# Row gathers of an edge stage released by another table, in a ring of 49 slots instead of 40

## The chip, the core and the metric

One core of a Trainium2 chip runs the kernel. The metric is the time of one execution on the device in microseconds (us). Engines are named as in the profile: PE is the matrix engine (TensorE), PEld its weight loads, DVE is VectorE, ACT is ScalarE, POOL is GpSimd, SP is SyncE, which here only issues transfers (DMAs).

## The reference

A graph layer on 3125 nodes of 256 features with 50000 edges sorted by destination, then a mixer and a layer of 16 experts. What matters here is the graph part, cut to it:

```python
xn = layernorm(x)
h   = einsum('nf,hfd->hnd', xn, W)                      # 8 heads
e   = leaky_relu(a_s[:, src] + a_d[:, dst], 0.2)         # a score for each edge and head
# for each head h_h, e_h with its gate g_h:
m   = segment_max(e_h, dst)
ex  = exp(e_h - m[dst])
den = segment_sum(ex, dst)
out = segment_sum(h_h[src] * (ex / den[dst])[:, None], dst)
acc = acc + g_h * out
# + bias, residual, layernorm, Wo; + linear attention on xn; then top-2 of 16 experts, layernorm
```

The destinations are drawn as 3125 times a squared uniform number, so that small node numbers have many edges and large ones few: windows of 16 nodes at the high end hold a little over 100 edges each, the lowest one over 3000.

## The kernel before

**Stages.** (1) The node stage normalises x, computes projections and scores of the nodes, and writes for each node a row of 272 numbers to DRAM (`node_rows`: the features, a one, the source scores of 8 heads). Ahead of it DVE works out, from the ends of the edge chunks, the tables that the edge stage goes by. (2) The edge stage sums over the edges. (3) A third stage reads the sums back and applies W, the layernorm and the expert choice. (4) The experts, and (5) an end.

**The edge stage, about 155 to 861 us.** The 50000 edges, from the highest destination down, are cut into 391 chunks of 128. A window is 16 nodes. A step is one chunk against one window: 586 steps, in 37 groups of 16 (592). Where nodes have few edges a chunk crosses into the next window often (some 1.8 steps for each chunk at the start), where they have many it rarely does (about 1.0 at the end). So a group uses 8 to 9 new chunks at the start and 14 to 15 at the end.

- POOL gathers the rows of each chunk's 128 source nodes by an indirect DMA (L735, 391 of them) into a slot of the ring `rows`, chunk number modulo `RING` = 40. `FLY` = 4 are in flight; before gather k POOL waits until gather k-4 has landed and counts it in `fetched` (L726), and then until the semaphore `prod`, which counts finished products, has reached `free_at[k]` (L732 to L734).
- ACT's `copy_as` (L907 to L914) waits on `fetched` for the last chunk of a group and copies the 16 scores' columns out of `rows` (`asb`). It runs two groups ahead of the products.
- ACT, DVE and PE turn these into exponentials by a chain of small steps, one group ahead. DVE's `spread` (L816, two per group) multiplies them out into the weights `pw`.
- PE's `product` (L1045, a step in two passes) multiplies `pw` with the chunk's rows into one of four PSUM banks `pO`; DVE's `accumulate` (L832, one per step, 592) adds it to the step before and keeps it in `acc`. PE needs the bank that DVE frees. SP stores `acc` to DRAM (L1131), 8 steps at a time in 4 parts, out of three buffers.

On each engine the order of the work is written out by hand: `groups([...])` lists stages with their lag in groups, and each engine runs through its list. There is no scheduler.

**When a gather is released.** `ends[:, 1, j]` is the number of the last step that uses chunk j, `ends[:, 2, j]` is j. PE adds 2 groups (32) to `prod` before its first product, and 1 at the start. The table is made at L491 to L493 of the node stage by DVE, on one partition: gather k may go when the product of step (last step of chunk k-4) - 48 is done (`LEAD` = 48), and not before the last product that uses chunk k-40, whose slot it takes. Some gathers at the start need no product at all.

**The read-back of maxima.** At the end of the edge stage SP loads the maxima of all steps into `ml` (L1146), and DVE makes `has` and `mm_` of them (L859, L860), which PE turns (L1093) and DVE scans. `ml`, `has` and `mm_` are buffers of their own for the whole edge stage, 5.8 KB in each partition. `gad`, of the same shape as `mm_`, is only used at the stage's start, and `picks`, of 900 numbers, only from stage 3 on.

## Time and profile before

| | us |
|---|---|
| median of three runs | 1581.97 |
| the three runs | 1574.44, 1581.97, 1582.84 |
| the profiled execution, its time | 1577.83 |
| its span in the trace | 1575.5 |
| node stage, to the first gather | 0 to 155.5 |
| edge stage, first product to last | 191 to 852 |
| third stage | about 865 to 1236 |
| experts, and the end | about 1236 to 1575 |

The stages follow each other; a stage cannot start before the data of the one before it is in DRAM. So the length of the edge stage goes into the total as it is. The profile cuts time into windows and tells for each engine the busy time and the number of instructions; in the edge stage POOL's count is the number of gathers, since it does nothing else there.

### The profile page before, as it was taken

Reading aid. Unit: us, or ns where it says so; the run is one execution under the profiler, and the core shown is the slowest. Engines: PE = TensorE matmul, PEld = TensorE weight load, DVE = VectorE, ACT = ScalarE, POOL = GpSimd, SP = SyncE. Lnnn points to the kernel's source line nnn. Section 1 sums busy time; section 2 is a strip of 40 time slices with the busy share of each in tenths; the row PEclk is TensorE's granted clock in tenths of the full one; section 3 lists DMA queues with packets and bytes.
Section 4 is the critical chain, followed back from the end, with each engine's and each line's share of the span. In section 5 each row is a group of like instructions: output and inputs, shape, how many; then the busy total and the mean of one; then the engine's idle time right before and its main releaser. Section 6 shows DMA issues by size and latency. Waiting matters only on the chain. (4 is left out here: it accounts for less than half of the span.)

```text
span 1575.5 us, 31018 instructions
## 1 busy us (share of the span) xinstructions
PE 1209.0 (77%) x6344; PEld 975.2 (62%) x6345; DVE 1004.9 (64%) x2859; ACT 504.2 (32%) x1977; POOL 690.7 (44%) x784
## 2 busy tenths in 40 slices
PE   4996689898888777677666299999991699999700
PEld 4774466666665555554444298888871689999600
DVE  6555378887777656666567468989975234444367
ACT  3452233332332222221121446555531123232200
POOL 1001655555556556556640246767663011111264
PEclk9998599999999888777888599999995799999955
DMA  5142677777777667666656833334323972222155
GB/s 184 46 88 79 131 214 231 223 234 220 218 230 224 195 189 216 193 203 191 175 178 165 262 117 134 134 133 141 133 72 118 325 252 70 70 70 70 61 163 153
DMA packets 219593, 256.19 MB, mean 163 GB/s; under 512 B 57269, under 2 KB 193336, under 8 KB 216024
## 3 DMA queue, kind: packets, MB, share of 16 engines
q1 hardware_dynamic: 177464, 140.79, 28.4%
q0 software_dynamic: 31088, 104.05, 23.0%
q10 hardware_dynamic: 10928, 10.12, 2.1%
q8 instruction: 37, 0.61, 0.2%
q14 instruction: 76, 0.62, 0.1%
HBM read 139.95 MB, written 114.93 MB: 162 GB/s over the span
## 5 line engine op out<-in xcount | busy, mean ns | idle before, releaser
L735 POOL DMA_INDIRECT rows<-node_rows,srcT x391 | 389.0, 995 | 272.4 <-PE pO L1045 132.6
L1045 PE MATMUL pO<-rows,pw 128*128 x1184 | 352.7, 428 | 67.5 <-issue 31.1
L832 DVE SCALAR_TENSOR_TENSOR acc<-acc,rsc,pO 128x257 f32<-128x257 f32 x592 | 281.7, 476 | 140.4 <-PE pO L1045 51.4
L1045 PEld LDWEIGHTS pO<-rows,pw 128*128 128x128 f32 x1184 | 223.1, 209 | 120.6 <-issue 93.1
L1377 PE MATMUL pW_<-W_again,aT 128*128 128x256 f32 x800 | 181.5, 380 | 0.4 <-DVE res L1444 0.4
L1377 PEld LDWEIGHTS pW_<-W_again,aT 128*128 128x128 f32 x800 | 148.7, 191 | 18.8 <-DVE res L1444 0.5
L1865 POOL DMA_DIRECT2D ys_rows<-ye x66 | 35.8, 542 | 235.5 <-DVE ye L1816 235.5
L1755 ACT ACTIVATE hT<-pHe,b 128x128 f32<-128x128 f32 x264 | 75.5, 368 | 188.3 <-PE pHe L1781 172.0
L1781 PEld LDWEIGHTS pHe<-xeT,w1e 128*128 128x128 f32 x1056 | 131.0, 196 | 7.1 <-DVE w1e L1806 2.8
L1781 PE MATMUL pHe<-xeT,w1e 128*128 128x128 f32 x1056 | 131.7, 279 | 3.2 <-DVE xeT L1799 3.2
L1790 PE MATMUL pYe<-w,hT 128*128 x528 | 125.4, 380 | 2.1 <-issue 1.3
L1428 DVE SCALAR_TENSOR_TENSOR own<-AG,al,own 128x256 f32<-128x256 f32 x200 | 111.1, 570 | 7.6 <-ACT own L1314 3.6
L1790 PEld LDWEIGHTS pYe<-w,hT 128*128 128x128 f32 x528 | 95.3, 191 | 13.4 <-issue 3.1
L914 ACT ACTIVATE asb<-rows 128x8 f32 x592 | 75.7, 209 | 75.9 <-issue 37.8
L816 DVE TENSOR_TENSOR pw<-pexp,eq 128x1024 f32<-128x1024 f32 x74 | 87.1, 1219 | 0.0
L1314 ACT ACTIVATE own<-xna,al 128x256 f32 (+1 forms) x200 | 82.2, 500 | 3.6 <-DVEq L1553 3.6
L1366 PE MATMUL pa<-cst,own 128*128 128x128 f32 x400 | 53.7, 292 | 36.7 <-DVE own L1428 36.7
L1799 DVE COPY xeT<-pXe 128x256 f32<-128x256 f32 x66 | 28.1, 425 | 84.3 <-PE pXe L1771 84.3
L1806 DVE COPY w1e<-w 128x1024 f32 x66 | 45.8, 694 | 51.8 <-issue 42.0
L1366 PEld LDWEIGHTS pa<-cst,own 128*128 128x128 f32 x400 | 49.2, 154 | 38.3 <-issue 33.9
L1288 POOL DMA_INDIRECT xs_rows<-ysc,slot_x x50 | 50.2, 1003 | 23.7 <-issue 11.3
L1874 POOL DMA_INDIRECT w1e<-ys_rows,slot x50 | 48.4, 968 | 25.4 <-issue 15.6
(332 smaller groups left out, 1968.3 us busy)
## 6 DMA issues: line engine op xcount, KB each, us to landing
agg_rows<-acc SPq DMA_DIRECT2D x296, 256.0 KB
w<-in_ffn_w SPq DMA_DIRECT2D x32, 512.0 KB, 5.6
xe<-xs_rows ACTq DMA_DIRECT2D x66, 128.0 KB, 2.1
ys_rows<-ye POOLq DMA_DIRECT2D x66, 128.0 KB, 2.0
rows<-node_rows,srcT POOLq DMA_INDIRECT x391
node_rows<-xna SPq DMA_DIRECT2D x25, 136.0 KB
xna<-in_x SPq DMA_DIRECT2D x5, 640.0 KB, 11.7
mix_rows<-hx SPq DMA_DIRECT2D x25, 128.0 KB
```

The source lines that it names most:

```text
L735: pool.indirect_dma_start(rows[:, k % RING, :], None, node_rows[:, :], at_row(srcT[:, k:k + 1])).then_inc(s_rows[k % len(s_rows)], 16)
L816: dve.tensor_tensor(pw[:, i, :, :].rearrange("p s (d h) -> p s d h", h=H), pexp[:, g % V2, s, :].unsqueeze(2).to_broadcast([P, HG, DW, H]) ...
L832: dve.scalar_tensor_tensor(out=acc[:, k % V3, s % HG, 0:D + 1], in0=before, scalar=rsc[:, g % V2, s:s + 1], in1=pO[n % PB][:, 0:D + 1], op ...
L914: ins = act.activation(asb[:, g % V2, s, :], rows[:, ds(at[s], 1), AS:AS + H].rearrange("p c h -> p (c h)"), ACT.Copy)
L1045: pe.matmul(pO[n % PB][:, 0:D + 1], pw[:, s // HG, s % HG, :], rows[:, ds(at[s % 4], 1), 0:D + 1].rearrange("p c f -> p (c f)"), start=Tru ...
L1314: ins = act.activation(own[:, c, h, :], tile(xna, t, 0, D), ACT.Copy, scale=al[:, 1, t, h:h + 1] if isinstance(t, int) else al[:, 1, ds(t, ...
L1366: mm = pe.transpose(pA[i][:, k * P:(k + 1) * P], own[:, c, n // KD, (n % KD) * P:(n % KD + 1) * P], ident)
L1377: mm = pe.matmul(pW[:, 0:D], aT[:, c, n, :], W[:, n % KD, n // KD, :], start=(n == 0), stop=(n == H * KD - 1))
L1428: ins = dve.scalar_tensor_tensor(out=own[:, c, h, :], in0=AG[:, c, h, :], scalar=al[:, 0, t, h:h + 1] if isinstance(t, int) else al[:, 0, ...
L1755: ins = act.activation(hT[:, c % 2, f, :], pH[c % 2][:, f * P:(f + 1) * P], ACT.Relu, bias=b1[:, ds(e, 1), f:f + 1].rearrange("p e f -> p ...
L1781: mm = pe.matmul(pH[c % 2][:, f * P:(f + 1) * P], w1e[:, c % S3, k, f * P:(f + 1) * P], xeT[:, c % 2, k, :], start=(k == 0), stop=(k == KD ...
L1790: mm = pe.matmul(pY[c % 2][:, 0:D], hT[:, c % 2, f, :], of_expert(w2, e, f), start=(f == 0), stop=(f == FK - 1))
```

## The change

The ring gets 49 slots. The table is made by three operations where there was one: each chunk takes a quarter of a step off the release, so that gather k may go when the product of step (last step of chunk k-4) - 48 - (k-4)/4 is done. The rule on the slot stays, now with chunk k-49. To make room `ml` and `has` stand in `picks` and `mm_` stands in `gad`. The slot numbers come from the same table made on the host, modulo 49.

```diff
-RING, FLY, LEAD, AHEAD = 40, 4, 48, 2
+RING, FLY, LEAD, AHEAD = 49, 4, 48, 2
+EARLIER = 0.25
...
-                    line.do(dve.tensor_scalar(may_go[:, FLY:CHUNKS], ends[:, 1, 0:CHUNKS - FLY], float(2 + AHEAD * G - LEAD), 1.0, ALU.add, ALU.max))
+                    line.do(dve.tensor_scalar(may_go[:, FLY:CHUNKS], ends[:, 2, 0:CHUNKS - FLY], -EARLIER, float(2 + AHEAD * G - LEAD), ALU.mult, ALU.add))
+                    line.do(dve.scalar_tensor_tensor(out=may_go[:, FLY:CHUNKS], in0=may_go[:, FLY:CHUNKS], scalar=0.0, in1=ends[:, 1, 0:CHUNKS - FLY], op0=ALU.add, op1=ALU.add))
+                    line.do(dve.tensor_scalar(may_go[:, FLY:CHUNKS], may_go[:, FLY:CHUNKS], 1.0, None, ALU.max))
                     line.do(dve.scalar_tensor_tensor(out=may_go[:, RING:CHUNKS], in0=ends[:, 1, 0:CHUNKS - RING], scalar=2.0 + AHEAD * G, in1=may_go[:, RING:CHUNKS], op0=ALU.add, op1=ALU.max))
                     line.do(dve.tensor_copy(free_at[:, FLY:CHUNKS], may_go[:, FLY:CHUNKS]))
...
-            ml = sb("ml", [P, SJ, DW, H + 1], ctx=ctx)
-            has = sb("has", [P, SJ, DW], ctx=ctx)
-            mm_ = sb("mm", [P, SJ, P], ctx=ctx)
+            spare = picks[:, :, :].rearrange("p t r -> p (t r)")
+            ml = spare[:, 0:SJ * DW * (H + 1)].rearrange("p (j d c) -> p j d c", d=DW, c=H + 1)
+            has = spare[:, SJ * DW * (H + 1):SJ * DW * (H + 2)].rearrange("p (j d) -> p j d", d=DW)
+            mm_ = gad
```

No engine's order changes; what changes in it stands on DVE, early in the node stage, ahead of `steps_in`, for which PE waits. `may_go` is the table before it is rounded into `free_at`. Before:

```order
L488 TENSOR_SCALAR rowc<-cs 128x5
L491 TENSOR_SCALAR may_go<-ends 1x387
L492 SCALAR_TENSOR_TENSOR may_go<-ends,may_go 1x351
L493 CAST free_at<-may_go 1x387
L495 TENSOR_TENSOR cs<-cs 128x5
```

and now:

```order
L489 TENSOR_SCALAR rowc<-cs 128x5
L492 TENSOR_SCALAR may_go<-ends 1x387
L493 SCALAR_TENSOR_TENSOR may_go<-may_go,ends 1x387
L494 TENSOR_SCALAR may_go<-may_go 1x387
L495 SCALAR_TENSOR_TENSOR may_go<-ends,may_go 1x342
L496 CAST free_at<-may_go 1x387
L498 TENSOR_TENSOR cs<-cs 128x5
```

Two operations on one partition have come in between; all else on every engine stands in the same row. How many gathers are released while a group's products run, worked out from the two tables and the drawn destinations:

| products of groups | 0-3 | 4-7 | 8-11 | 12-15 | 16-19 | 20-23 | 24-27 | 28-31 | 32-33 | 34-36 |
|---|---|---|---|---|---|---|---|---|---|---|
| before (28 need no product) | 34 | 35 | 37 | 40 | 42 | 46 | 48 | 52 | 28 | 1 |
| now (32 need no product) | 39 | 41 | 39 | 38 | 40 | 43 | 47 | 52 | 20 | 0 |

## Rows read from the trace of the kernel before

**Rows 1.** The page: busy time of each engine, and the chain that ended last.

```profile
PE 1209.0 (77%) x6344; PEld 975.2 (62%) x6345; DVE 1004.9 (64%) x2859; ACT 504.2 (32%) x1977; POOL 690.7 (44%) x784
...
PE 16%; issue 2%; DVE 2%; DMA 1%; DVEq 1%; POOL 1%; ACTq 0%; ACT 0%; SPq 0%; POOLq 0%
```

**Rows 2.** Windows of four groups each (the last two: two and three), busy us.

```profile
core 0: us, PE busy (x) PEld busy (x) DVE busy (x) ACT busy (x) POOL busy (x), PEclk, DMA share, GB/s
191.00:258.70 67.70, 59.20 (x280) 42.53 (x279) 51.35 (x140) 21.00 (x118) 39.05 (x39) 0.96 0.73 212
258.70:322.10 63.40, 57.47 (x277) 41.56 (x277) 51.65 (x140) 21.30 (x123) 35.21 (x35) 0.97 0.77 228
322.10:387.50 65.40, 57.80 (x278) 41.54 (x277) 51.52 (x141) 21.14 (x119) 37.87 (x37) 0.97 0.76 222
387.50:454.60 67.10, 58.19 (x277) 41.11 (x276) 51.41 (x140) 21.40 (x122) 38.92 (x40) 0.97 0.76 225
454.60:529.10 74.50, 59.47 (x278) 42.72 (x277) 51.56 (x141) 22.43 (x126) 42.85 (x43) 0.92 0.73 220
529.10:606.80 77.70, 63.80 (x264) 45.33 (x263) 51.25 (x136) 20.47 (x115) 46.19 (x46) 0.85 0.67 196
606.80:684.60 77.80, 55.08 (x221) 40.35 (x221) 49.44 (x124) 18.16 (x105) 47.72 (x49) 0.81 0.70 206
684.60:769.40 84.80, 57.63 (x221) 41.15 (x221) 50.04 (x124) 17.48 (x103) 49.67 (x52) 0.76 0.64 189
769.40:814.80 45.40, 27.78 (x112) 20.32 (x111) 24.75 (x62) 9.28 (x55) 27.02 (x28) 0.80 0.68 200
814.80:852.30 37.50, 30.88 (x138) 21.86 (x137) 30.37 (x73) 6.86 (x38) 0.95 (x1) 0.96 0.53 131
```

**Rows 3.** Waits of DVE in the second window: total, times, longest, us.

```profile
DVE acc L832 <- PE pO L1045: 3.5, 5, 2.0
```

**Rows 4.** The same view in the eighth window, 684.6 to 769.4 us.

```profile
DVE acc L832 <- remote: 9.0, 5, 2.4
DVE acc L832 <- PE pO L1045: 8.3, 9, 2.6
```

**Rows 5.** Groups of instructions, 191 to 852 us: busy, mean ns, idle before and releasers.

```profile
L735 POOL DMA_INDIRECT rows<-node_rows,srcT x368 | 365.7, 994 | 260.4 <-PE pO L1045 132.6 <-issue 95.2 <-remote 18.1
```

**Rows 6.** Timeline of POOL around 760 us: start, duration, what, idle before and releaser.

```profile
759.08 0.95 POOL L735 DMA_INDIRECT rows<-node_rows,srcT  x1 [0.30 <-issue]
760.33 0.95 POOL L735 DMA_INDIRECT rows<-node_rows,srcT  x1 [0.31 <-issue]
```

**Rows 7.** Timeline of DVE at the same place.

```profile
759.81 0.48 DVE L832 SCALAR_TENSOR_TENSOR acc<-acc,rsc,pO 128x257 f32<-128x257 f32 x1 [1.14 <-remote]
762.66 0.48 DVE L832 SCALAR_TENSOR_TENSOR acc<-acc,rsc,pO 128x257 f32<-128x257 f32 x1 [2.37 <-remote]
765.55 1.07 DVE L832 SCALAR_TENSOR_TENSOR acc<-acc,rsc,pO 128x257 f32<-128x257 f32 x2 [2.40 <-remote]
```

**Rows 8.** Timeline: gather of chunk 350, and copies that need it.

```profile
750.31 0.95 POOL L735 DMA_INDIRECT rows<-node_rows,srcT  x1 [1.08 <-PE pO L1045]
...
767.73 1.95 ACT L914 ACTIVATE asb<-rows 128x8 f32 x16 [1.93 <-POOLq L726]
```

**Rows 9.** Timeline of POOL at the stage's start.

```profile
199.00 1.03 POOL L735 DMA_INDIRECT rows<-node_rows,srcT  x1 [2.31 <-remote]
```

**Rows 10.** Timeline of DVE and PE in the node stage.

```profile
17.43 0.35 DVE L491 TENSOR_SCALAR may_go<-ends 1x387 f32<-1x387 f32 x1
17.81 0.51 DVE L492 SCALAR_TENSOR_TENSOR may_go<-ends,may_go 1x351 f32<-1x351 f32 x1
...
22.15 1.05 PE L401 MATMUL pT<-by_tile,cst 128*128 128x25 f32 x4 [12.47 <-DVEq L506]
```

**Rows 11.** Windows of one group each, the first and the second.

```profile
192.00:212.60 20.60, 16.14 (x71) 11.49 (x70) 12.93 (x35) 3.94 (x22) 11.44 (x12) 0.89 0.58 167
212.60:227.80 15.20, 14.17 (x71) 10.08 (x70) 12.77 (x35) 5.50 (x32) 9.04 (x9) 1.00 0.79 228
```

## The prediction, made before the changed kernel was run

> **What bounds the kernel now.** I read the page first. The chain that ended last only reaches back through the experts [rows 1], so it tells nothing of the edge stage, where the change works; but the stages follow each other, and what the edge stage gains or loses goes into the total. So I read that stage by windows, four groups of products each [rows 2]. Every window does the same work: 64 steps, the same number of accumulations and of small operations. The reader is to see that the same work takes 63.4 us in the second window and 84.8 us in the eighth. DVE is busy 51.7 and 50.0 us in them: it is the engine nearest to being full at first, and stands idle later. The granted clock goes from 0.97 to 0.76, a mix of the two levels, 2.4 and 1.2 GHz; it falls after PE has stood idle, so it follows the waits more than it makes them. What does change with the window is the number of gathers: 35 against 52.
>
> Who waits for whom? In the second window DVE's accumulate waits 3.5 us for products, in the eighth 8.3, and 9.0 more for something that the profile can't name [rows 3, 4]. Is it for gathered rows? No: the gather of chunk 350 is issued at 750.31 us, and the copies of the first group that needs it run at 767.73 [rows 8], 17 us later. The wait of ACT that the row names on POOL is 1.93 us, on a counter which had long passed what that chunk needs. And POOL waits for products 132.6 us in all [rows 5], so it could go faster than it is let. Nobody visibly waits for a gather; yet with many gathers the steps are slower. The timeline shows the form of it: POOL issues gathers every 1.25 us, as at 759.08 and 760.33 [rows 6], and meanwhile DVE's accumulates come 2.9 us apart instead of 0.9, again released by what has no name [rows 7]. SP stores nothing in those 6 us, so it isn't the stores. I take it that a gather costs the rest of the stage something by being there, by a mechanism that I can't name.
>
> **What a gather costs, from the windows.** From the second window to the eighth: (84.8 - 63.4) / (52 - 35) = 1.26 us for each gather. The ninth has two groups; doubled, 56 gathers and 90.8 us, on the same line (63.4 + 21 x 1.26 = 89.9). The last has three groups; by four thirds, 1 gather and 50.0 us. From there to the second it is (63.4 - 50.0) / (35 - 1) = 0.39 us for each [rows 2]. The fourth window, 40 gathers, is at (67.1 - 63.4) / 5 = 0.74 for each above the second. So gathers are cheap up to some 35 in four groups and get dear above 40. The first window, 39 gathers in 67.7 us, lies on the dear line (63.4 + 4 x 1.26 = 68.4). But that is its first group's doing, 20.6 us with 12 gathers, in which everything starts; the second takes 15.2 with 9 [rows 11], which is no more than the second window's mean of 15.9.
>
> **The change part by part.**
> The number of gathers is 391 in both. The change moves them, as the table of releases shows: four more need no product, 5 more go in groups 0 to 3, 6 more in 4 to 7, 2 more in 8 to 11; then 2, 2, 3 and 1 fewer in the four windows to group 27, none in 28 to 31, 8 fewer in 32 and 33, 1 fewer after. That the table is right for before is seen in the counts, 35, 37, 40, 43, 46, 49, 52, 28 and 1 against 35, 37, 40, 42, 46, 48, 52, 28 and 1 [rows 2].
>
> Early. At 199.00 POOL issues gather 28, the first that had to wait [rows 9]: the 4 more that need no product come right there, so there are 4 + 5 = 9 more in the first window. Cheap they are +3.5 us, dear +11.3. I take the middle, +7.4, because four of them fall into the crowded first group and five into groups that have had 9 in 15.2 us. In 4 to 7, 6 more, and in 8 to 11, 2 more, come on top of 35 and 37, where the line turns: between 0.74 and 1.26 each, I take 1.0, +6.0 and +2.0. Early together +15.4, between +6.6 (all 17 at 0.39) and +21.4 (all at 1.26).
>
> Middle and late. 8 fewer at 1.26: -10.1 us. In groups 28 to 31 nothing changes: there the slot decides in both kernels, and the ring of 49 shifts all releases by nine chunks and leaves their rate. In 32 and 33, 20 instead of 28: that is the density of the fourth window, whose half is 33.6 us, instead of 45.4: -11.8. The last one: -0.4. Together -22.3. If the middle's slowness comes from something other than the count, its 10.1 aren't given back: then -12.2.
>
> DVE's table. Two more operations: one like L492 (0.51 us for 351 numbers, so some 0.56 for 387), one like L491 (0.35), each with the 0.03 us between dependent ones. They stand ahead of the matmul at 22.15 us for which PE had waited 12.47 us [rows 10], and PE's row of W and the normalised tiles hang on it, so they are on the path: +0.9 us, between 0 (if a later wait for x or W hides them) and 1.
>
> The buffers. `ml` and `has` in `picks`, `mm_` in `gad`: the same instructions with the same shapes and the same waits, at other addresses. `picks` is free until the third stage, `gad` has been read by the SP transfer that DVE waits for at its first group. Nothing added, 0.
>
> What is late next where a gather's cost goes? The small chain of a group and DVE's own 12.8 us of work in it; the last window shows that floor, 12.5 us for a group with hardly a gather [rows 2].
>
> Sum: 15.4 - 22.3 + 0.9 = -6.0 us. The profiled execution took 1577.83, so 1571.8, and I say 1572. That execution lies 4 us under the median of the three runs, of which one is at 1574.44; a measured pair may well differ from my sum by 3 us for that alone.
>
> **A rule weighed against it.** The row first: a gather takes POOL 950 ns where nothing holds it [rows 6], and the mean is 994 [rows 5]; so POOL is held up by (994 - 950) x 368 = 16 us over the stage, off the path, since it idles 260 us. The Trainium skill says (SBUF — State Buffer, section "SBUF: two separate sides") that engines and DMAs reach SBUF by separate ports and can't slow each other, and that the only pair that shares is VectorE with GpSimd. By that rule a gather may stretch on POOL but costs PE nothing, and moving gathers moves nothing; the trace doesn't agree as I read it, since the windows' times follow the count of gathers. The sum by the rule is the second rival below.
>
> **The rivals.**
> *It does better* (the early gathers are cheap): in the windows to group 11, DVE has waits of 3.5 us [rows 3] and POOL idle time in plenty, and the extra 17 gathers fill it at 0.39 us, +6.6, the late ones come off as above: -22.3 + 6.6 + 0.9 = -14.8, so 1563. For it: the second group with 9 gathers in 15.2 us [rows 11]; four such would be 36 in 60.8. Against it: the fourth window's 0.74 and the first one's 67.7 us.
> *The count is not the cause* (by the row on POOL alone, gathers are hidden wherever they stand; the later windows are slow for another reason, such as PE's lower clock after each pause, which is as early as before): the moves cancel, only DVE's table stays, 1577.8 + 0.9 = 1579. For it: no wait in the profile names a gather. Against it: the last window, the same work, at once 12.5 us for a group when the gathers end.
> *It gets slower*: the early gathers run back to back. With 9 more, 48 gathers are due in 67.7 us, and POOL at 1.25 us each does them in 60, so it runs nearly without a pause, as around 760 us, where a step takes 2.9 us. PE pays the dear price in the first window too (+11.3), which makes early +21.4, and the middle isn't relieved, since its windows stay above 35: 21.4 - 12.2 + 0.9 = +10.1, so 1588. It decides where the free time of POOL between gathers in the first eight groups falls to nothing; with 35 gathers in 63.4 us it still has 28 us, with 41 it has 22.
> *It doesn't do what it says*: the gathers can't follow the earlier release. That would need POOL at its limit before, and it isn't [rows 5]. I give it no chance of its own.
>
> **How the numbers follow.** Forecast 1572: 0.47. Better, 1563: 0.26. No effect, 1579: 0.14. Slower, 1588: 0.13. A measurement of this kernel can tell about 0.5%, 8 us, from no change. The forecast lies near that bound, at -6; of its 0.47 I put 0.10 beyond it. So faster by over 0.5% is 0.36, slower 0.12, the rest, 0.52, within. Range: 1562 to 1586, from the better case to the near side of the slower one, with the case of no effect inside.
>
> **What would show it.** In the profile after, windows of four groups: 73 to 77 us in the first and 67 to 71 in the second (before 67.7 and 63.4), with some 48 and 41 gathers; 72, 74, 77 in the fifth to seventh; the pair of groups 32 and 33 at 34 instead of 45.4 us, and the last three at 37. The first gather should start 0.9 us later, near 156.4. If the first two windows keep their time with more gathers, the better case holds; if the middle keeps 74.5 to 77.8 with fewer, the count isn't its cause. I'm wrong altogether if copies of ACT in fact waited for gathers: then the ring of 49 would take more off the late windows than any sum here.

## The result, and the profile after

The changed kernel took 1592.61 us (median of 8 runs), the kernel before 1582.01 in its 8 runs beside it: a ratio of 1.007, with a 95% interval of 1.0039 to 1.0102. It is slower by 0.7%. The forecast was 1572, and the sign is wrong. One of the 8 runs of the changed kernel took 3074.57 us, as a few runs of other kernels did later; such runs count in the medians and not in the ratios. The profiled execution of the kernel after took 1598.69 us (span 1596.4), against 1577.83 of the kernel before: +20.9 us, twice the +10.6 of the medians, so single terms of a few us below are not safe on this pair alone.

The same windows as in [rows 2], of the kernel after (four groups each, then two and three; the last line is the first group alone, as in [rows 11]):

```profile
190.80:274.60 83.80, 67.18 (x278) 48.12 (x276) 51.11 (x140) 20.57 (x113) 46.71 (x48) 0.83 0.64 185
274.60:347.10 72.50, 58.26 (x277) 41.16 (x277) 51.72 (x141) 21.39 (x122) 41.53 (x42) 0.98 0.72 213
347.10:417.80 70.70, 59.03 (x276) 41.98 (x276) 51.28 (x141) 21.24 (x121) 39.00 (x39) 0.95 0.71 209
417.80:480.10 62.30, 55.63 (x277) 39.98 (x277) 51.30 (x141) 21.35 (x122) 37.43 (x38) 1.00 0.80 236
480.10:548.50 68.40, 56.46 (x276) 40.00 (x276) 51.24 (x141) 21.49 (x119) 36.93 (x40) 1.00 0.73 218
548.50:625.30 76.80, 60.00 (x263) 42.16 (x263) 51.03 (x137) 21.77 (x122) 43.61 (x45) 0.89 0.69 205
625.30:702.90 77.60, 55.77 (x220) 40.11 (x220) 49.35 (x125) 18.05 (x108) 47.33 (x48) 0.81 0.68 202
702.90:787.70 84.80, 52.76 (x221) 38.59 (x221) 49.64 (x125) 17.68 (x106) 51.67 (x53) 0.80 0.66 194
787.70:829.40 41.70, 29.53 (x110) 20.27 (x110) 24.77 (x63) 8.99 (x50) 21.30 (x22) 0.78 0.61 183
829.40:869.90 40.50, 34.25 (x138) 24.71 (x138) 30.88 (x74) 7.72 (x45) 0.00 (x0) 0.87 0.56 141
190.80:219.50 28.70, 20.41 (x69) 14.40 (x67) 12.49 (x35) 4.91 (x27) 18.10 (x19) 0.70 0.55 153
```

Read the length of each window (the number behind its range) against that of before, and the count of POOL, which is the gathers. DVE is busy 51 us in the first five windows, as before. Its work hasn't changed; the idle time beside it has. Window by window:

| groups | before | after | change | forecast | gathers before, after |
|---|---|---|---|---|---|
| 0-3 | 67.7 | 83.8 | +16.1 | +7.4 | 39, 48 |
| 4-7 | 63.4 | 72.5 | +9.1 | +6.0 | 35, 42 |
| 8-11 | 65.4 | 70.7 | +5.3 | +2.0 | 37, 39 |
| 12-27 (four windows) | 297.1 | 285.1 | -12.0 | -10.1 | 178, 171 |
| 28-31 | 84.8 | 84.8 | 0.0 | 0 | 52, 53 |
| 32-33 | 45.4 | 41.7 | -3.7 | -11.8 | 28, 22 |
| 34-36 | 37.5 | 40.5 | +3.0 | -0.4 | 1, 0 |

The first three windows take 30.5 us more and all the later ones together 12.7 less, so the stage is longer by 17.8 us. The first group alone takes 28.7 us instead of 20.6, with 19 gathers instead of 12. (The row of before opens 1 us after its first product. From the first product of this group to the first of the next it is 29.1 us against 21.0, the same 8.1 more, with 6 more gathers.) Who waits there? DVE's waits in the first window of after:

```profile
DVE acc L836 <- PE pO L1049: 13.9, 12, 4.7
DVE acc L836 <- issue: 10.1, 5, 5.1
```

and the same of before (191 to 258.7 us), first its unnamed and then its named one:

```profile
DVE acc L832 <- issue: 6.4, 5, 5.1
DVE acc L832 <- PE pO L1045: 4.0, 3, 2.5
```

"issue" and "remote" stand where the profile can name no releaser. The 5.1 us are the wait for the stage's first product, in both kernels. Of the 16.1 us more, 13.6 are waits of the accumulate in these rows. The form is that of [rows 6] and [rows 7], now at the stage's start. POOL's timeline of after, and DVE's in the same stretch:

```profile
206.19 0.95 POOL L739 DMA_INDIRECT rows<-node_rows,srcT  x1 [0.30 <-issue]
207.44 0.95 POOL L739 DMA_INDIRECT rows<-node_rows,srcT  x1 [0.30 <-issue]
208.89 0.94 POOL L739 DMA_INDIRECT rows<-node_rows,srcT  x1 [0.50 <-issue]
210.50 0.94 POOL L739 DMA_INDIRECT rows<-node_rows,srcT  x1 [0.67 <-issue]
```

```profile
206.85 0.48 DVE L836 SCALAR_TENSOR_TENSOR acc<-acc,rsc,pO 128x257 f32<-128x257 f32 x1
...
212.67 0.48 DVE L836 SCALAR_TENSOR_TENSOR acc<-acc,rsc,pO 128x257 f32<-128x257 f32 x1 [4.74 <-PE pO L1049]
```

While POOL runs gather after gather, the accumulate stands still for 4.74 us. By itself this stretch doesn't show who holds up whom: the next gather, at 213.49, waits for a product too (2.05 us). ACT's `pexp`, which needs another result of PE, starts at 212.58, after a wait of 6.09 us with no named releaser, and so within 0.1 us of the accumulate. What is late is thus more than one product.

How many such stalls there are can be counted in DVE's timeline. Waits of the accumulate of 1 us and more, after the one for the first product:

| groups | 0-3 | 4-7 | 8-11 | 12-15 | 16-19 | 20-23 | 24-27 | 28-31 | 32-33 | 34-36 | sum |
|---|---|---|---|---|---|---|---|---|---|---|---|
| before: number | 2 | 1 | 2 | 3 | 4 | 7 | 7 | 8 | 5 | 0 | 39 |
| before: us | 3.5 | 2.0 | 3.9 | 5.6 | 7.9 | 16.9 | 13.7 | 15.5 | 10.1 | 0 | 79 |
| after: number | 8 | 5 | 2 | 1 | 4 | 8 | 6 | 6 | 2 | 0 | 42 |
| after: us | 15.7 | 8.0 | 7.4 | 2.0 | 7.2 | 15.7 | 14.9 | 15.3 | 5.1 | 0 | 91 |

In these two traces the stalls are many where the gathers are many; in groups 0 to 7, where the change puts 16 gathers more, 3 have become 13. So the rival named "it gets slower" has the place right.

### The profile page after: what moved, and what is told of

Its sections match the earlier page's. It is cut to its first block and busy times, and to the rows that moved or that the text cites. A ratio compares the mean times of both kernels' runs of the same rounds, so it can differ in the third digit from the quotient of the medians.

```text
span 1596.4 us, 31020 instructions
## 1 busy us (share of the span) xinstructions
PE 1212.7 (76%) x6344; PEld 974.1 (61%) x6345; DVE 1005.6 (63%) x2861; ACT 504.4 (32%) x1977; POOL 690.8 (43%) x784
## 5 line engine op out<-in xcount | busy, mean ns | idle before, releaser
L1318 ACT ACTIVATE own<-xna,al 128x256 f32 (+1 forms) x200 | 82.2, 499 | 3.6 <-DVEq L1557 3.6
L1878 POOL DMA_INDIRECT w1e<-ys_rows,slot x50 | 48.7, 974 | 26.5 <-issue 13.6
```

The costliest lines, as they stand in the source:

```text
L1318: ins = act.activation(own[:, c, h, :], tile(xna, t, 0, D), ACT.Copy, scale=al[:, 1, t, h:h + 1] if isinstance(t, int) else al[:, 1, ds(t, ...
```

## The experiments

The runs came in jobs; in each, a few kernels ran on one chip beside runs of the kernel before. One thing must be said ahead, since no number below can be read without it: the kernel before did not always take the same time. In the first measurement and in the two jobs after it it took 1582, 1594 and 1579 us; in the three later jobs 1509, 1512 and 1510. One chip had both, 1579 in one job and 1512 in a later one, so this is no property of a chip. I call them the 1580 condition (that of the prediction) and the 1510 condition. What makes them I don't know. The traces tell them apart: the part behind the edge stage takes 722 to 733 us in the profiled executions of the first and 710 to 717 in those of the second, and accumulates that wait for 1 us or more, past the first product, occur only in the first. Ratios compare within a job alone; windows set beside each other from different jobs are good to a few us only.

### One part of the change at a time (1580 condition)

Only the quarter step, ring of 40 and buffers as before:

```diff
+EARLIER = 0.25
-                    line.do(dve.tensor_scalar(may_go[:, FLY:CHUNKS], ends[:, 1, 0:CHUNKS - FLY], float(2 + AHEAD * G - LEAD), 1.0, ALU.add, ALU.max))
+                    line.do(dve.tensor_scalar(may_go[:, FLY:CHUNKS], ends[:, 2, 0:CHUNKS - FLY], -EARLIER, float(2 + AHEAD * G - LEAD), ALU.mult, ALU.add))
...
```

> The release table of the change alone: a quarter step per chunk earlier, ring of 40 as before, `ml`, `has`, `mm_` in buffers of their own. Theory A (what costs is the number of gathers that fall on a group of products): the table releases 41, 39 and 38 ... no, worked out: 39 in groups 0-3, 36 in 4-7, 36 in 8-11 and as after from there on, so the first window of four groups is as long as after (83 us, before 66.6), the second and third lie near before (64 to 68), the last windows as before: total 8 to 14 us above before. Theory B (a larger ring costs, by its addresses or by the chunks that lie ready): all windows as before within 3 us, total as before within 3 us.

Measured: 1597.22 against 1594.47, ratio 1.0025 (0.9995 to 1.0055). Its first window:

```profile
194.40:279.10 84.70, 64.63 (x278) 47.51 (x277) 51.05 (x140) 20.31 (x112) 44.50 (x46) 0.85 0.61 180
```

84.7 us with 46 gathers: the dear first window is the doing of the table, and it comes again in a second kernel. The second and third windows took 65.0 and 63.7 us here, but with 36 gathers in each: the ring of 40 lets no more go, where the changed kernel had 42 and 39. So this kernel doesn't test the +9.1 and +5.3 of the pair above.

Only the ring of 49, with its buffers:

```diff
-EARLIER = 0.25
+EARLIER = 0.0
```

> The ring of 49 and the moved buffers, with the quarter step set to 0 (three table operations stay). Theory A: releases are those of before up to chunk 265 or so, so the first six windows of four groups keep their time within 3 us; groups 25 to 32 take up to one or two gathers more each and get slower, groups 33 on have fewer and get faster; total within 5 us of before. Theory B (a larger ring costs): the early windows are longer too, total +10 us as after.

Measured: 1598.72, ratio 1.0022 (0.9995 to 1.0049). The first window is 66.8 us; the eighth:

```profile
695.10:785.80 90.70, 59.53 (x221) 41.95 (x221) 49.48 (x125) 18.15 (x106) 55.22 (x57) 0.74 0.65 191
```

57 gathers and 90.7 us, against 52 and 84.8 [rows 2]: 1.18 us for each one more, the line that the prediction drew. But those two windows are of different jobs. The next kernel, of the same job, has 54 gathers and 85.4 us there, which makes 1.8 us for each one more:

```profile
688.20:773.60 85.40, 55.67 (x220) 39.89 (x220) 49.82 (x125) 18.08 (x109) 51.63 (x54) 0.79 0.66 196
```

Only the buffers and the two more operations on DVE:

```diff
-RING, FLY, LEAD, AHEAD = 49, 4, 48, 2
-EARLIER = 0.25
+RING, FLY, LEAD, AHEAD = 40, 4, 48, 2
+EARLIER = 0.0
```

> Only the moved buffers and the two more table operations: ring 40, quarter step 0. Theory A: total as before, at most +1 us; first product at 192 us as before and after. Theory C (the read-back's buffers or the table operations cost the 3 us that the span of after has more than its edge stage explains): +3 us.

Measured: 1595.22, ratio 0.9991 (0.997 to 1.0012). These parts cost nothing that can be measured. Set beside the kernel with the early table, it also shows what moving gathers does within one job: the first window is 16.4 us longer with the early table (84.7 against 68.3, 46 gathers against 40), and the four windows of groups 12 to 27 are 10.1 us shorter (290.5 against 300.6, 171 gathers against 179). That leaves table and ring; each alone lies at +0.2%, and neither is resolved from zero, so how the 0.7% divides between them stays open.

### Does a gather cost anything at all? (1580 condition)

Every second gather is left out, and its chunk is read from the slot of the one before, so this kernel computes something else. POOL waits for no landing of a gather that isn't there, so at most two are in flight instead of four, and no two of them start closer than 1.9 us:

```diff
-                        pool.indirect_dma_start(rows[:, k % RING, :], None, node_rows[:, :], at_row(srcT[:, k:k + 1])).then_inc(s_rows[k % len(s_rows)], 16)
+                        if k % 2 == 0:
+                            pool.indirect_dma_start(rows[:, k % RING, :], None, node_rows[:, :], at_row(srcT[:, k:k + 1])).then_inc(s_rows[k % len(s_rows)], 16)
...
```

> Before, with every second gather left out: an odd chunk's products read the rows of the chunk before it (the result is another one), POOL still waits on the table for each chunk, ACT, PE, DVE and SP do all their work. Theory A: with 17 to 28 gathers for four groups instead of 35 to 56 all windows fall to 55 to 62 us, and the late ones lose their excess: the edge stage shrinks by 70 to 100 us, from 661 to about 575. Theory D (the late windows are slow for another reason than gathers, such as PE's clock or the stores): the early windows keep 63 to 67 us and the late ones stay above 75, total less than 20 us down.

Measured: 1479.25, ratio 0.9265 (0.9227 to 0.9302): 115 us for 195 gathers, 0.59 us each. Its fourth and eighth windows:

```profile
369.30:428.60 59.30, 55.37 (x276) 40.44 (x276) 51.24 (x141) 21.03 (x121) 19.09 (x20) 1.00 0.68 211
614.10:677.50 63.40, 50.44 (x221) 37.12 (x221) 49.61 (x125) 17.34 (x106) 24.07 (x26) 0.88 0.65 195
```

84.8 us have become 63.4 with half the gathers, though POOL had idled 260 us before [rows 5]. So gathers do cost the others time, and the rival by which the late windows are slow for another reason falls. Whether it is their number or their being four at a time this kernel can't tell, since it changes both; the kernel with two in flight below takes that further. What has gone is seen in DVE's waits of this kernel over the whole stage, 191 to 755 us (total, times, longest):

```profile
DVE acc L834 <- PE pO L1047: 19.8, 56, 0.5
DVE acc L834 <- issue: 13.5, 39, 0.7
```

No accumulate waits longer than 0.7 us any more; in [rows 4] a wait reaches 2.6.

### Is it what POOL or PE does beside a gather? (1580 condition)

Two suspects were the registers that POOL and PE load to know a gather's release and a step's slot. For POOL the releases stand as constants in the program, worked out on the host:

```diff
-                            steps = pool.value_load(free_at[0:1, k:k + 1], min_val=1, max_val=(GROUPS + AHEAD) * G + 1)
-                            pool.wait_ge(prod.sem, steps)
+                            pool.wait_ge(prod.sem, FREE[k])
```

> Before, with the release of each gather as a constant in POOL's wait instead of a number that POOL's sequencer loads from SBUF and waits on in a register. The gathers, their releases and all other work are the same. Theory A1 (what disturbs PE is the gather itself, its transfer or the making of its descriptors): total as before within 4 us, the eighth window stays near 85 us. Theory A2 (the disturbance is POOL's sequencer, which loads a register from SBUF and polls `prod` for each gather): the late windows fall towards 65 to 70 us, total 40 us or more down.

Measured: 1575.56 against 1578.65, ratio 0.9959 (0.9927 to 0.9992). For PE the slots:

```diff
-                                    at[:] = nc.values_load_multi_w_load_instructions(step_tab[0:1, g, s:s + 4], engines=(mybir.EngineType.PE,), min_val=0, max_val=RING - 1,
-                                                                                  skip_runtime_bounds_check_because="a chunk's slot")[1]
...
-                                pe.matmul(pO[n % PB][:, 0:D + 1], pw[:, s // HG, s % HG, :], rows[:, ds(at[s % 4], 1), 0:D + 1].rearrange("p c f -> p (c f)"),
+                                pe.matmul(pO[n % PB][:, 0:D + 1], pw[:, s // HG, s % HG, :], rows[:, CHUNK[n] % RING, 0:D + 1],
```

> Before, with the slots of PE's products as constants, so that PE's sequencer loads nothing from SBUF and computes no address. Theory A1: as before within 6 us, perhaps some us faster. Theory A3 (PE stalls because its own loads of slot numbers are held up while POOL issues gathers): the pauses of 2.9 us vanish, the eighth window falls from 85 to about 65 us, total 60 us or more down.

Measured: 1574.4, ratio 0.9957 (0.9927 to 0.9987). The eighth windows, first of the kernel with POOL's constants, then with PE's:

```profile
694.70:776.00 81.30, 58.97 (x220) 42.03 (x220) 49.44 (x125) 16.95 (x102) 51.59 (x51) 0.75 0.68 196
```

```profile
681.60:766.30 84.70, 58.51 (x220) 42.50 (x221) 49.82 (x125) 16.78 (x97) 50.49 (x52) 0.74 0.65 189
```

Each saves 0.4%, and the windows stay at 81 to 85 us: the register loads are not what gathers cost. (The first of these executions was the longest of its ten, 1587.26, with its first product only at 204.1 us.)

### The release later, and fewer in flight (1580 condition)

```diff
-RING, FLY, LEAD, AHEAD = 40, 4, 48, 2
+RING, FLY, LEAD, AHEAD = 40, 4, 40, 2
```

> Before with a release 8 steps later (LEAD 40 instead of 48), the opposite of the change. Theory A: 4 or 5 fewer gathers in the first window and somewhat fewer where the table decides, so the first window goes from 67 to 60 to 63 us; the ones left over come later, where the slot rule mattered, a gather or two more in each late window. Total 0 to 6 us down. Rival: copies of ACT come to wait for rows, since the lead is now under the 48 steps by which they run ahead: then each window gets longer, total up.

Measured: 1594.21, ratio 1.008 (1.004 to 1.0119). The first and the eighth window:

```profile
192.30:255.80 63.50, 57.66 (x278) 42.07 (x276) 50.80 (x140) 20.39 (x113) 32.32 (x33) 0.96 0.70 207
695.30:778.20 82.90, 59.08 (x221) 41.94 (x221) 49.78 (x125) 18.18 (x109) 51.78 (x52) 0.77 0.66 196
```

The first is 4.2 us cheaper with 6 gathers fewer, with no stall of 1 us left in it, and the whole is slower all the same: the sixth window takes 82.8 us and groups 32 and 33 take 51.1, against 77.7 and 45.4 [rows 2]. The rival of the expectation, copies of ACT that come to wait for rows, doesn't show: between 200 and 800 us such a wait takes 1.8 us at most. Moving releases later was no gain either.

```diff
-RING, FLY, LEAD, AHEAD = 40, 4, 48, 2
+RING, FLY, LEAD, AHEAD = 40, 2, 48, 2
```

> Before with two gathers in flight instead of four. Theory A1 in the form that it is the closeness of gathers in time: with two in flight POOL can't issue one each 1.25 us unless one lands in 2.5 us, so gathers spread out, and the first group (20.6 us) and the late windows get shorter; total 5 to 20 us down. In the form that each gather costs its share whenever it comes: no change, within 4 us. Rival: two in flight are too slow, the copies of ACT wait for rows and the late windows get longer.

Measured: 1843.25, ratio 1.1648 (1.16 to 1.1696). Its eighth window, and ACT's wait for rows between 200 and 800 us:

```profile
857.60:978.70 121.10, 55.42 (x221) 39.36 (x221) 49.73 (x125) 17.39 (x104) 50.78 (x52) 0.68 0.45 134
```

```profile
ACT asb L914 <- POOLq L726: 198.8, 23, 13.2
```

52 gathers take 121.1 us, 2.33 us each: with two in flight a gather's own time from issue to landing sets the pace, and `asb`, ACT's copy out of the rows, is where it shows.

The same trace settles more. The waits of DVE's accumulate after the first product, 200 us to the end of the stage:

```profile
DVE acc L832 <- PE pO L1045: 33.1, 104, 0.9
DVE acc L832 <- issue: 16.3, 45, 0.7
```

All 391 gathers are made, and in a job of the 1580 condition, yet no accumulate waits 1 us or more, and no wait of DVE is put down to "remote". In the two kernels with constants, of the same job and with four in flight, accumulates wait up to 5.4 us. So the stalls don't follow from the number of gathers alone: with two in flight, whether half of the gathers are made or all, they are gone. Two in flight also spreads the gathers out (never three in a row at 1.25 us), and nothing here separates the two. The way out costs more than it saves, since the rows then come too late.

### The other condition: both kernels again

The same two kernels once more, unchanged, in the 1510 condition. First the kernel before, measured against further runs of itself:

> The kernel before once more, for a profile of it on the chip of this job. The three comparisons so far had it at 1579 and 1594 us, and at 1509 us on the last job's chip: the chips differ in what a gather costs. Theory A (stalls by gathers, of a size that depends on the chip): near 1580, windows as first shown; near 1510, the first six windows of four groups at 60 us whatever the gathers, and late windows at 65 to 80 us with waits of ACT's copies for gathers.

Measured: 1511.65 against 1511.73, ratio 1.0006 (0.9986 to 1.0026).

> The changed kernel once more, beside b2. On a chip where before takes near 1580: 8 to 14 us slower than it, as measured. On one where it takes near 1510: the early windows stay at 60 us with more gathers, and the ring of 49 ends waits of ACT's copies in groups 24 to 35, so it is 10 to 25 us faster than before.

Measured: 1504.36, ratio 0.9956 (0.9932 to 0.998); and once more in the last job:

> The changed kernel for the third time. Its ratio to before was 1.007 where before took 1582, and 0.9956 where it took 1512. If before is near 1580 here: 1.007 within 0.004; if near 1510: 0.996 within 0.003.

1504.47 against 1509.94, ratio 0.9957 (0.9935 to 0.998). **In this condition the change is faster by 0.4%.** The rows of the kernel after are of the first of these two jobs, from the longest of its eleven executions (1516.76); the profiled one of the other job (1502.16) has 60.9, 59.6 and 79.1 us in the same windows. First the kernel before (second and eighth window, DVE's and ACT's waits in 590 to 800 us), then the kernel after (first, second, eighth, ACT's wait):

```profile
251.60:311.20 59.60, 55.95 (x276) 40.34 (x276) 51.20 (x141) 21.08 (x121) 34.80 (x36) 1.00 0.80 240
628.60:711.70 83.10, 56.03 (x220) 39.83 (x220) 49.71 (x125) 17.39 (x104) 54.47 (x57) 0.77 0.68 201
```

```profile
DVE zT L765 <- ACT zlow L925: 44.1, 10, 9.2
DVE acc L832 <- PE pO L1045: 10.7, 35, 0.5
```

```profile
ACT asb L914 <- POOLq L726: 53.0, 9, 9.7
```

```profile
191.30:252.00 60.70, 56.63 (x277) 41.01 (x275) 50.59 (x140) 20.27 (x113) 40.48 (x40) 0.98 0.79 234
252.00:311.90 59.90, 55.93 (x277) 40.09 (x277) 51.36 (x141) 21.19 (x122) 38.09 (x38) 1.00 0.81 245
627.80:710.00 82.20, 55.11 (x221) 39.39 (x221) 49.55 (x125) 17.39 (x104) 54.67 (x56) 0.77 0.70 204
```

```profile
ACT asb L918 <- POOLq L730: 51.5, 9, 10.5
```

Here the early windows take 60 us whatever the number of gathers in them, 36, 38 or 40, and no accumulate waits over 0.5 us for a product in the late stretch of the rows above. The late windows gain less: the sixth takes 65.0 us and the seventh 73.4, against 77.7 and 77.8 [rows 2], and the eighth is nearly as long as it was, 83.1 against 84.8, by another wait: ACT's copies wait up to 9.7 us for rows, and DVE's `zT` waits for ACT behind them. Over the whole stage (190 to 860 us) that wait of ACT's is, in the kernel before of the first measurement and in the kernel before here:

```profile
ACT asb L914 <- POOLq L726: 31.7, 20, 2.3
```

```profile
ACT asb L914 <- POOLq L726: 94.7, 30, 9.7
```

57 gathers in 83.1 us are 1.46 us each. I take that as the pace of four in flight, too slow for what the steps use up from the sixth window on. The next experiment tests it.

### More in flight (1510 condition)

If the pace of four sets the late windows, more semaphores, and nothing else, must shorten them. The table stays as it is; two pairs of semaphores are used twice over to find room, with their counts moved by one load:

```diff
-            s_rows = [sem(f"s_rows{c}") for c in range(FLY)]
-            s_flg, s_top = [sem(f"s_flg{c}") for c in range(V2)], sem("s_top")
+            s_rows = [sem(f"s_rows{c}") for c in range(8)]
+            s_flg, s_top = s_x[0:2], sem("s_top")
...
```

> Before with eight gathers in flight instead of four, the same release table. Two in flight took 2.4 us for each gather, so some 4.7 us from issue to landing; four give 1.2 us if that stays, and the late windows of before show 1.62 us for each gather. Theory L (the pace of gathers at four in flight is what the late windows follow): with eight the late windows fall from 85 towards 65 to 70 us, total 40 us down. Theory A (each gather disturbs the others' work, POOL waits for releases and not for landings): total within 6 us of before.

Measured: 1494.16 against 1509.03, ratio 0.9899 (0.9882 to 0.9915), and again 1495.94, 0.9899 (0.9867 to 0.9931):

> Before with eight gathers in flight, once more. On a chip near 1510: 1494 as measured, 1% faster. On a chip near 1580: theory A, POOL waits for landings little and gathers closer together stall PE more, so within 6 us of before; theory L (the pace of four in flight): 30 us or more faster.

The same edit on the changed kernel:

> The changed kernel with eight gathers in flight, the candidate to beat both. On a chip near 1510: 15 us under f8b or more, about 1480, since ACT's copies no longer wait. On a chip near 1580: as after within 6 us.

Measured: 1478.15, ratio 0.9804 (0.9754 to 0.9854); its seventh and eighth windows, and its wait of ACT in 606 to 761 us:

```profile
548.30:609.30 61.00, 48.35 (x220) 35.08 (x220) 49.28 (x125) 17.50 (x107) 42.26 (x43) 0.94 0.83 247
609.30:673.50 64.20, 51.99 (x220) 37.69 (x220) 49.40 (x125) 16.11 (x94) 45.03 (x47) 0.86 0.80 238
```

```profile
ACT asb L918 <- POOLq L730: 21.4, 5, 9.1
```

The eighth window falls from 82.2 to 64.2 us. With a ring of 49 and the earlier table, eight in flight lie 2.0% under the kernel before and 1.7% under the changed kernel; with ring and table of before they lie 1.0% under it. The waits of ACT in the last row fall in the groups from 32 on; in the two windows shown it waits at most 1.7 us for rows. Repeated, and with `range(6)` for `range(8)`:

> The changed kernel with eight gathers in flight, once more. If before takes near 1510 in this job: 1478 as measured, 2% faster. If it takes near 1580 or more: PE is stalled by gathers as in the first profiles, so near the changed kernel, 1590 within 10 us.

1479.24 against 1509.94, ratio 0.9792 (0.9751 to 0.9832).

> The changed kernel with six gathers in flight: a chunk is counted as landed two gathers sooner than with eight, which matters in the last groups, where the 49 slots are just the 48 steps by which ACT's copies run ahead. Near 1510: the pace of gathers is no limit any more (4.7 us over 6 is under 1.25 us), so as f8a2 or up to 6 us faster by the groups 31 to 35. Theory L with a latency that grows with load: 5 to 10 us slower than f8a2.

Six: 1478.13, ratio 0.978 (0.9741 to 0.9818). Six in flight are as good as eight. Both beat the kernels before and after by 2.1 and some 1.7% in this condition. In the 1580 condition no kernel with more than four in flight was run.

### What a gather's cost hangs on: bytes, traffic or the gather (1510 condition)

Odd gathers fetch rows of 32 bytes instead of 1088, to a buffer of their own, so POOL does all 391 (like the next kernel, this one computes something else):

```diff
-                        pool.indirect_dma_start(rows[:, k % RING, :], None, node_rows[:, :], at_row(srcT[:, k:k + 1])).then_inc(s_rows[k % len(s_rows)], 16)
+                        if k % 2 == 0:
+                            pool.indirect_dma_start(rows[:, k % RING, :], None, node_rows[:, :], at_row(srcT[:, k:k + 1])).then_inc(s_rows[k % len(s_rows)], 16)
+                        else:
+                            pool.indirect_dma_start(tiny[:, k % FLY, :], None, ad_rows[:, :], at_row(srcT[:, k:k + 1])).then_inc(s_rows[k % len(s_rows)], 16)
...
```

> As e_half, but for the 195 odd chunks POOL issues a gather of 128 rows of 8 numbers (32 bytes a row, out of the table of destination scores) into a small tile of its own: as many gathers, descriptors and waits as before, and half of the bytes. (The result is another one, as in e_half.) Theory A-count (a gather costs by its issue: the descriptors that POOL makes and the engines fetch): total back to before within 15 us. Theory A-bytes (it costs by its transfer): total as in e_half, some 110 us under before, plus 20 us at most.

Measured: 1494.87 against 1509.03, ratio 0.9892 (0.9865 to 0.9918). And the kernel without the odd gathers, again with at most two in flight, and with 185 plain loads of the same size on SP in their stead:

```diff
+                                if q < 3 - i:
+                                    n = 5 * g + 3 * i + q
+                                    if n >= 3:
+                                        sp.wait_ge(s_plain[n % 3], 16 * (n // 3) + 16)
+                                    sp.dma_start(plain[:, n % 3, :], node_rows[n % NT * P:(n % NT + 1) * P, :]).then_inc(s_plain[n % 3], 16)
...
```

> As e_half, with 5 plain loads a group on SP's queue (185 in all) of 128 rows of 1088 bytes, the size of a gather, into a spare tile: nearly the bytes of before into SBUF, without POOL and its descriptors. Theory A-count: as e_half within 20 us. Theory A-bytes (traffic as such): near before, 90 us or more above e_half.

Measured: 1482.9, ratio 0.982 (0.9803 to 0.9836). The eighth windows, of the small rows and of the plain loads:

```profile
616.20:694.50 78.30, 56.49 (x220) 40.08 (x220) 49.59 (x125) 17.39 (x104) 55.10 (x56) 0.76 0.57 165
```

```profile
612.10:681.50 69.40, 53.64 (x220) 39.14 (x220) 49.54 (x125) 17.39 (x104) 25.93 (x27) 0.83 0.74 225
```

With half the bytes and all the gathers 78.3 us remain of the 83.1 that the kernel before takes in the next job; with nearly all the bytes and half the gathers 69.4. 56 gathers in 78.3 us are 1.40 us each, against 1.46. So the pace of four in flight hangs on the number of gathers far more than on their bytes. The second kernel says less than the first, since no kernel with half the gathers and no loads was run in this condition. Both runs were meant for the stalls of the 1580 condition; they fell into the other, where no product stalls, so on the cause of those stalls they say nothing.

## Why the prediction was wrong

**The sum, term by term.** On the profiled pair: early +30.5 instead of +15.4, a miss of 15.1; groups 12 to 27 -12.0 instead of -10.1, a miss of -1.9; groups 32 and 33 -3.7 instead of -11.8, +8.1; the last three +3.4; DVE's table and the start of the stage -0.2 instead of +0.9, -1.1; what follows the stage +3.3. These are 26.9, the distance from -6.0 to +20.9. About 10 us of the 20.9 are spread of the two executions.

**The step that failed: the price of the early gathers.** The first window was put at +7.4 for 9 gathers, the middle between cheap and dear. It cost 16.1, 1.8 us each, above even the dear price of 1.26. The kernel with the early table alone shows it again. Over the eight profiled kernels of the 1580 condition with four in flight and all gathers, the first window takes 61.9, 63.5, 66.8, 67.7, 68.2, 68.3, 84.7 and 83.8 us for 34, 33, 38, 39, 40, 40, 46 and 48 gathers: about 0.8 us for each up to 40, and some 2.3 for each above (an estimate, over different jobs). The prediction had the row for it and read it away: the first window of before lay on the dear line, and that was laid to "everything starts" there. And it averaged: 9 more in a window of 67.7 us was taken as a density, while the four that need no product come in one run from 199.7 us on, back to back, as in [rows 6]. The first group, into which they fall, took 8.1 of the 16.1; the other half fell into the next three groups, so that run explains half at most. Of the second and third windows' +14.4, against a forecast of +8.0, only the profiled pair speaks, since no other kernel of this condition had 42 gathers in the second. What those windows cost is not settled.

**The second: what groups 32 and 33 give back.** "That is the density of the fourth window, whose half is 33.6 us" is wrong. 22 gathers took 41.7 us. Over the same eight kernels these two groups take 41.7, 40.5, 45.4, 42.9, 45.4, 42.6, 50.9 and 51.1 us for 22, 23, 28, 28, 29, 29, 33 and 34 gathers, about 0.9 us for each, not the 1.48 that the term implied.

**The third: the mechanism was half seen.** That "a gather costs the rest of the stage something by being there" holds with four in flight and in one condition. With two in flight 391 gathers stall nothing, and in the 1510 condition neither do four or eight. The count stood for this only as long as nothing else changed.

**What was right.** That windows with more gathers are slower, in the 1580 condition; the return in the middle (-12.0 in the pair, -10.1 between two kernels of one job); nothing in 28 to 31; the buffers at nothing. DVE's table: PE's wait at the start of the node stage is

```profile
22.99 1.05 PE L402 MATMUL pT<-by_tile,cst 128*128 128x25 f32 x4 [13.19 <-DVEq L509]
```

0.84 us later than in [rows 10], as forecast. But the first product comes at 190.8 us against 191.0, so nothing of it shows there. Kernels with the same operations had it at 191.3 (buffers) and 195.2 (ring), so the start itself varies by more than this term.

**Of the rivals**, "it gets slower" named the place, and its 1588 is 4.6 under the median. That size is luck: it put early at +21.4, the middle at nothing and groups 32 and 33 at -11.8, where the pair shows +30.5, -12.0 and -3.7. It got 0.13 of the chances, because I let a middle price stand where the first window's own row should have decided. Its free time of POOL, 28 and 22 us, counts 1.0 us for each gather; at the 1.25 us used in the same place it is 20 and 12.

**"Nobody visibly waits for a gather"** holds for both kernels of the pair (waits of 2.3 us at most that the profile puts down to rows) and fails in the 1510 condition, where ACT waits 53.0 us in the late windows. The prediction's last sentence named this as what would make it wrong altogether. It also said that the ring of 49 would then take more off the late windows than any sum there; with four in flight it took 0.9 and 4.0 us off the eighth in two executions. There the change comes out at -0.44%; its parts were not run apart in that condition, so which of them it comes from is open.

**The rule weighed against it** (the Trainium skill, SBUF — State Buffer, section "SBUF: two separate sides": engines and DMAs don't slow each other). In the 1580 condition leaving out 195 gathers takes 115 us off while POOL idles, which that rule doesn't lead one to expect; by what path a gather holds up a product no run shows. With two in flight it holds up none in that same condition. In the 1510 condition 36, 38 and 40 gathers in a window leave it at 59.6 to 60.7 us, and there the trace agrees with the rule.

**Open.** What makes the two conditions. What stalls the products in the first, the register loads being excluded: closeness in time is not shown to be the trigger, since around the stalls of before POOL issues 0.54 gathers for each us, as in the whole stage (0.55); it can't be told from this either, as a stalled product holds back the next gather. How three or six in flight would do there.

## What to carry to other kernels

Where a transfer costs its neighbours, don't take one price for it: in the first window here the price went from 0.8 to 2.3 us for each gather at 40. Price moved work in the window that it makes densest, by that window's own row. Leaving work out to see what it costs also changes how much of it is in flight; vary the two apart. A prefetch has three knobs, the release, the room and the number in flight; find by the consumer's longest wait which one holds, since in the 1510 condition ring and earlier release together were worth 0.4% with four in flight and 1.0% with eight (0.9804 against 0.9899). A change of half a percent should be measured on more than one occasion: here its sign depended on it.

## What the runs showed of the hardware that was not expected

- One program took 1579 to 1594 us (medians) in three jobs and 1509 to 1512 in three others, on one and the same chip too. Within a job it repeated to 0.1% (b2). Of the 65 us between the two profiled executions 53 are in the edge stage and 12 behind it: the early windows are at 60 us instead of 63 to 68, with no product late by more than 0.5 us after the first window. The last three groups are the other way round, 37.5 us and then 46.2: one copy of ACT waits 9.7 us for rows there and DVE's `zT` 9.2 us behind it, where in the first execution DVE waits 1.1 us at most.
- In the slower condition accumulates waited up to 5.6 us beside gathers with four in flight (LEAD 40), and 0.9 us at most with two, all 391 gathers made.
- Indirect gathers of 128 rows of 1088 bytes: 2.33 us each with two in flight, 1.46 with four; with eight they are no longer the bound of the seventh and eighth windows, where ACT waits at most 1.7 us for them. POOL issues them 1.25 us apart.
- With four in flight, 32-byte rows in every second gather left the late window at 78.3 of 83.1 us.
